# A float32 attention chain on one core: moving the first layer's softmax normalisation behind the product with the values

## The chip, the cores and the metric

The kernel runs on one core of a Trainium2 chip. The metric is the device time of one execution in microseconds (us); lower is better. Everything is float32. A large product is made of three passes of matmuls: each operand is split into a high part (type fp32r) and the low rest, and high times high, high times low and low times high are added up.

## The reference

Four sequences of 512 tokens of width 512 go through three blocks (16 tiles of 128 rows on the chip):

```python
# layer 0: grouped-query attention, 32 query heads of 16 columns, 8 key/value heads, blocks of 128 keys
attn = softmax(q @ k.T / 4 + mask)          # float32, over the 128 keys
x = layernorm((attn @ v) @ Wo + bo + x) * gamma + beta
# layers 1 and 2: x = x + cross_attention(layernorm(x), ctx)   (16 heads of 128 columns, one bias key and value)
# then the MLP:   x = x + gelu(layernorm(x) @ W1 + b1) @ W2 + b2
```

Only layer 0 is changed. Dividing the weights by their sum ahead of the product with `v` or dividing the product behind it gives the same result.

## The kernel before, in words

The 16 row tiles are worked off in two halves of 8 tiles (`hf` = 0, 1); each half goes through layer 0, the two cross-attention layers and the MLP. The program is written out by hand per engine (`@block.tensor`, `.scalar`, `.vector`, `.gpsimd`, `.sync`); each engine's queue runs strictly in the order written, and semaphores tie the queues together. No planner is involved.

**Layer 0 of a half** has 8 units (`u`), each a group of 8 heads for 4 tiles, and so 32 steps (`s` = 0 to 31, `u = s // 4`). A step is one tile with 8 heads, a block of 128 rows by 1024 weights. It passes through the engines so:

- TensorE `s0_(s)` (L647 to L661, 12 matmuls) makes the scores in PSUM banks 2 to 5, columns 0 to 255 of each. There is one such buffer, so scores `s + 1` wait for `z0` of step `s`.
- VectorE `soft0(s)` adds the mask and copies the scores to one of four SBUF buffers (L1343, semaphore `z0`), and takes the negated maximum of each head (L1348).
- ScalarE `e0(s)` (L1059) takes the exponential of the first OWN = 5 heads, one instruction each (L1064, with the maximum as bias and the sum over the row accumulated). GpSimd `sub(s)` (L415) subtracts the maximum for the other 3 heads, and ScalarE then takes their exponential in one instruction (L1067).
- VectorE `rec0(s)` sums those 3 heads (L1353) and takes the reciprocals of the 8 sums (L1358).
- GpSimd `norm(s)` multiplies all 1024 weights by the reciprocals (L422).
- TensorE `t0(s)` transposes the 8 heads (L670), waiting for `norm`; ScalarE copies them out of PSUM (L1117); TensorE `pv0(s)` multiplies by the values (L683, 16 small matmuls) into one fourth of PSUM bank 1.
- After four steps of a unit, ScalarE adds the value bias and writes the high part of the contexts (L1075), VectorE the low part (`cxlo0`, L1362).
- TensorE `out0` (L688) multiplies the contexts by `Wo` into bank 0; VectorE adds the tile to `X` (`add0`, L1310). `q0(u)` (12 matmuls, L567) makes the next units' queries, whose two parts ScalarE (L1047) and VectorE (`qlo0`, L1335) write.

What each engine does in iteration `s` of its loop is fixed by hand. TensorE: `t0(s)`, `pv0(s-1)`, `s0_(s+4)`, then the extras named for `s` in `Q_AT` and `ROWS_AT`. ScalarE: the copy of `t0(s)`, then `e0(s+3)`. VectorE: `rec0(s+1)`, `cxlo0`, `qlo0`, `soft0(s+3)`, `add0`. GpSimd: `norm(s+1)`, `sub(s+3)`, then a row of the output bias (`BO_AT`, L456) and pieces of 256 columns of the weight slabs of later stages (`SPLIT_AT`): a copy (L385) and a subtraction (L446) each.

**The end of layer 0 in a half.** TensorE fills the last four iterations with the first keys and values of layer 1. VectorE takes the statistics of the first four rows (L1373), needs a square root of ScalarE (`root`, L1082, after a load of its table), finishes the layer norm (`own`, L1409 and L1407), adds the first values' bias (L1486) and takes new statistics (L1417), and writes the low part of the last contexts (L1362). Then TensorE runs the last 12 matmuls of `last_rows0` (L703), 48 matmuls of values and the transposes of the first rows of layer 1 (L789).

## Time and profile before

| | us |
|---|---|
| runs, median of 3 | 2455.49 (2453.92 to 2456.33) |
| profiled execution: own time | 2454.8 |
| its span | 2453.0 |
| TensorE busy | 2363.4 (96%) |
| VectorE busy | 1218.1 (50%) |
| ScalarE busy | 866.1 (35%) |
| GpSimd busy | 815.1 (33%) |

The profiled execution took 1.8 us more than its span and 0.7 us less than the median. A busy share is a mean over the span. In the 40 slices of the page TensorE stands at 9 tenths nearly everywhere, but layer 0 of either half (from about 25 to 200 us and from about 1240 to 1415 us) looks different from the rest: there VectorE, ScalarE and GpSimd stand at 7 to 10 tenths. For a change in layer 0 those two stretches are to be read, not the means.

### The profile page before, as it was taken

What the parts mean: (1) busy time and instruction counts of PE and PEld (TensorE: products, weight loads), DVE (VectorE), ACT (ScalarE), POOL (GpSimd) and SP (SyncE); (2) the same over time, 40 slices, a digit from 0 to 9 for tenths busy, and PEclk for the clock granted to TensorE, in tenths of its full rate; (3) what the DMA queues carried; (4) which work ended last, traced back from release to release, by engine and by line L of the source; (5) the groups of instructions that cost most, each with busy time, mean ns of one, the idle gap of its engine ahead of it and who ended that gap; (6) DMA issues with size and microseconds to landing.
All of it is one profiled execution on the core that took longest, in us unless ns stands there. A gap on an engine that the chain in (4) does not pass through costs nothing.

```text
span 2453.0 us, 38741 instructions
## 1 busy us (share of the span) xinstructions
PE 2363.4 (96%) x14768; PEld 2033.3 (83%) x14768; DVE 1218.1 (50%) x2041; ACT 866.1 (35%) x2499; POOL 815.1 (33%) x598
## 2 busy tenths in 40 slices
PE   6888999999999999999989899999999999999999
PEld 5677888888888898878867678888888888888887
DVE  6986333334533334466679853343354333434654
ACT  6964222222422222242369542222233222223321
POOL 5974222233422322230049542223243222322100
PEclk9999999999999999999999999999999999999999
DMA  4102101012110101211320021111111111110110
GB/s 179 36 10 82 35 34 60 34 43 67 41 35 34 43 34 35 81 43 52 107 96 10 10 82 36 42 51 43 51 57 35 35 43 34 43 51 13 61 43 35
DMA packets 37765, 120.08 MB, mean 49 GB/s; under 512 B 3616, under 2 KB 3872, under 8 KB 37664
## 3 DMA queue, kind: packets, MB, share of 16 engines
q1 hardware_dynamic: 37664, 118.69, 14.0%
q8 instruction: 68, 1.11, 0.2%
q14 instruction: 33, 0.27, 0.0%
HBM read 114.48 MB, written 4.19 MB: 48 GB/s over the span
## 4 chain that ended last, share of the span: by engine, by line
PE 84%; POOL 7%; DVE 3%; ACT 2%; issue 2%; DMA 1%; SPq 0%; POOLq 0%; DVEq 0%; ACTq 0%
PE PS L567 71%; PE PS L798 5%; PE PS L814 4%; PE PS L806 2%; POOL XN L422 1%; POOL W L446 1%; ACT AT L1137 1%; POOL X L456 1%; POOL XN L415 1%; POOL HF L422 1%; POOL P0D L422 1%; POOL W L385 1%; ACT PS L1137 1%; PE PS L789 1%; PE PS L834 0%
## 5 line engine op out<-in xcount | busy, mean ns | idle before, releaser
L567 PE MATMUL PS<-AT,W 128*128 128x512 f32 x2496 | 607.5, 394 | 7.1 <-DVE AT L1431 6.0
L567 PEld LDWEIGHTS PS<-AT,W 128*128 128x128 f32 x2496 | 471.3, 190 | 111.2 <-DVE AT L1431 8.2
L485 POOL TENSOR_TENSOR PR<-PR,RC 128x512 f32<-128x512 f32 x128 | 133.3, 1041 | 979.4 <-DVE RC L1516 979.4
L1310 DVE TENSOR_TENSOR X<-PS,X 128x512 f32<-128x512 f32 x416 | 286.0, 690 | 293.8 <-PE PS L567 286.6
L567 PE MATMUL PS<-CT,W 128*128 128x512 f32 x1632 | 411.1, 401 | 10.4 <-DVE CT L1305 10.4
L567 PE MATMUL PS<-W,CX 128*128 128x512 f32 x1632 | 397.1, 397 | 7.7 <-DVE Q L1335 4.1
L567 PE MATMUL PS<-W,CT 128*128 128x256 f32 x3072 | 385.8, 284 | 0.0
L567 PEld LDWEIGHTS PS<-W,CT 128*128 128x128 f32 x3072 | 372.9, 191 | 1.3 <-issue 0.8
L567 PEld LDWEIGHTS PS<-W,CX 128*128 128x128 f32 x1632 | 299.8, 188 | 75.0 <-issue 8.3
L567 PEld LDWEIGHTS PS<-CT,W 128*128 128x128 f32 x1632 | 300.5, 190 | 69.8 <-issue 11.0
L1164 ACT ACTIVATE CX<-PS,VEC 128x512 fp32r<-128x512 f32 x128 | 88.0, 688 | 660.7 <-PE PS L814 660.7
L1541 DVE TENSOR_TENSOR V<-PS,BVR 128x512 f32<-128x512 f32 x124 | 85.5, 691 | 397.1 <-PE PS L567 397.1
L1153 ACT ACTIVATE PR<-PS,MX 128x129 f32<-128x129 f32 x512 | 181.7, 370 | 179.9 <-DVE MX L1510 179.9
L378 POOL TENSOR_TENSOR W<-RAW,W 128x1024 fp32r<-128x1024 f32 (+1 forms) x101 | 240.3, 2379 | 8.4
L385 POOL TENSOR_SCALAR W<-RAW 128x1024 fp32r<-128x1024 f32 (+2 forms) x149 | 135.1, 907 | 263.3 <-PE PS L567 250.4
L1147 ACT ACTIVATE Q<-PS,BQS 128x512 f32<-128x512 f32 x128 | 88.0, 688 | 345.0 <-PE PS L567 345.0
L567 PE MATMUL PS<-W,HB 128*128 128x512 f32 x768 | 180.2, 390 | 0.1
L567 PEld LDWEIGHTS PS<-W,HB 128*128 128x128 f32 x768 | 143.8, 188 | 30.7 <-DVE X L1310 1.0
L1547 DVE SCALAR_TENSOR_TENSOR CX<-PS,VEC,CX 128x512 fp32r<-128x512 f32 x128 | 96.1, 751 | 131.5 <-ACT CX L1164 131.2
L798 PE MATMUL PS<-K,Q 128*128 128x129 f32 x1024 | 136.0, 276 | 2.6 <-ACT Q L1147 2.6
L814 PE MATMUL PS<-PT,V 128*128 128x128 f32 x1024 | 135.1, 275 | 1.4 <-ACT PT L1159 1.4
L814 PEld LDWEIGHTS PS<-PT,V 128*128 128x128 f32 x1024 | 129.3, 191 | 6.5 <-ACT PT L1159 1.8
(108 smaller groups left out, 2450.5 us busy)
## 6 DMA issues: line engine op xcount, KB each, us to landing
RAW<-in_wq SPq DMA_DIRECT2D x44, 512.0 KB, 4.3
RAW<-in_wo SPq DMA_DIRECT2D x44, 512.0 KB, 3.3
RAW<-in_wk SPq DMA_DIRECT2D x40, 512.0 KB, 3.2
RAW<-in_wv SPq DMA_DIRECT2D x40, 512.0 KB, 3.5
raw_c<-in_cT SPq DMA_DIRECT2D x8, 512.0 KB, 5.8
raw_x<-in_xT SPq DMA_DIRECT2D x8, 512.0 KB, 6.3
BVR<-in_bv_rows SPq DMA_DIRECT2D x8, 512.0 KB, 3.7
X<-in_x SPq DMA_DIRECT2D x4, 1024.0 KB, 11.5
```

The source lines that it names most:

```text
L378: eng.tensor_tensor(W[:, n, 1, 0:width], RAW[:, n, 0:width], W[:, n, 0, 0:width].bitcast(F32), ALU.subtract).then_inc(w_ready[n], 1)
L385: return nc.gpsimd.tensor_scalar(out, in_, 1.0, 0.0, ALU.mult, ALU.add)
L485: nc.gpsimd.tensor_tensor(PR[:, :, 0:P], PR[:, :, 0:P], RC[:, 0, 0:BT].unsqueeze(2).to_broadcast([P, BT, P]), ALU.mult).then_inc(norm_done, 1)
L567: ins = nc.tensor.matmul(out, lhs(c, a), rhs(c, b), start=(k == 0), stop=(k == total - 1))
L798: ins = nc.tensor.matmul(PS[:, BS + b // 2, b % 2 * 256:b % 2 * 256 + T1], Q[:, b * P:(b + 1) * P], K[:, h, b, 0:T1], start=True, stop=True)
L814: ins = nc.tensor.matmul(PS[:, BPV, b * P:(b + 1) * P], V[:, tb, b, h * P:(h + 1) * P], PT[:, b * P:(b + 1) * P], start=True, stop=True)
L1147: nc.scalar.activation(Q[:], PS[:, BA, :], ACT.Identity, bias=BQS[:, bass.ds(ly * H1 + head, 1)], scale=K1 ** -0.5).then_inc(q_ev, 1)
L1153: ins = nc.scalar.activation(PR[:, b, 0:T1], PS[:, BS + b // 2, b % 2 * 256:b % 2 * 256 + T1], ACT.Exp, bias=MX[:, 0, b:b + 1], accum_out= ...
L1164: nc.scalar.activation(CX[:, h, 0, :], PS[:, BPV, :], ACT.Identity, bias=VEC[:, bass.ds(cols + g * 2 + (COL_BIASV + h), 1)]).then_inc(cx_h ...
L1310: V_.tensor_tensor(X[:, tile, :], PS[:, bank, :], X[:, tile, :], ALU.add).then_inc(done, 1)
L1541: V_.tensor_tensor(V[:, tb, 2 * i:2 * i + 2, :], PS[:, BC + i, :].rearrange("p (b d) -> p b d", d=256), BVR[:, bass.ds(g * 256, 256)].unsq ...
L1547: V_.scalar_tensor_tensor(CX[:, h, 1, :], PS[:, BPV, :], VEC[:, bass.ds(cols + g * 2 + (COL_BIASV + h), 1)], CX[:, h, 0, :].bitcast(F32), ...
```

## The change

OWN goes from 5 to 4. `norm` is gone. TensorE transposes the weights as soon as `e0` has made them. GpSimd gets `half(s)`, which adds the two halves of each of the last 4 heads into 64 columns, and VectorE sums those. The reciprocals are written 16 times each, as 128 columns (`RC0`), TensorE transposes them (`rt0`) into columns 256 to 383 of a score bank, and once a unit VectorE multiplies the contexts by them (`cxnorm0`). ScalarE only copies the contexts out of PSUM (`cxraw0`); GpSimd splits them into two parts (`context`), and for the last unit ScalarE and VectorE do. The value bias is added to the values instead. VectorE's loop runs `rec0(s)` at its end instead of `rec0(s+1)` at its start, and adds a row between the two instructions of `soft0`. The tables of the extras are laid out anew; the first keys and values of layer 1, the statistics and the root each come one iteration later.

```diff
@@ -39,18 +39,18 @@
...
-OWN = 5
+OWN = 4
 BUFS0 = 4
 Q_AT = {0: 2, 3: 3, 8: 4, 12: 5, 16: 6, 20: 7}
-SPLIT_AT = {0: (3, (0,)), 1: (3, (1,)), 2: (3, (2,)), 3: (3, (3,)), 4: (0, (0,)), 5: (0, (1,)), 6: (0, (2,)), 7: (0, (3,)),
-            12: (2, (0,)), 13: (2, (1,)), 14: (2, (2,)), 15: (2, (3,)), 20: (1, (0, 1)), 21: (1, (2, 3)),
-            22: (3, (0,)), 23: (3, (1,)), 24: (3, (2, 3)), 25: (0, (0,)), 26: (0, (1,)), 27: (0, (2,)), 28: (0, (3,))}
+SPLIT_AT = {0: (3, (0,)), 1: (3, (1,)), 2: (3, (2,)), 3: (3, (3,)), 4: (0, (0, 1)), 6: (0, (2,)), 7: (0, (3,)),
+            11: (2, (0,)), 13: (2, (1,)), 15: (2, (2,)), 16: (2, (3,)), 17: (1, (0,)), 18: (1, (1,)), 20: (1, (2,)), 21: (1, (3,)),
+            24: (3, (0, 1)), 25: (3, (2, 3)), 26: (0, (0,)), 27: (0, (1,)), 28: (0, (2,)), 29: (0, (3,))}
 PIECES = sum(len(parts) for _, parts in SPLIT_AT.values())
-BO_AT = {8: 0, 9: 1, 10: 2, 11: 3, 16: 4, 17: 5, 18: 6, 19: 7}
-ROWS_AT = {9: (0, 0), 10: (0, 1), 11: (0, 2), 13: (0, 3), 17: (1, 0), 18: (1, 1), 19: (1, 2), 21: (1, 3),
-           25: (2, 0), 26: (2, 1), 27: (2, 2), 28: (2, 3)}
+BO_AT = {8: 0, 9: 1, 10: 2, 12: 3, 13: 4, 14: 5, 19: 6, 20: 7}
+ROWS_AT = {10: (0, 0), 11: (0, 1), 14: (0, 2), 15: (0, 3), 18: (1, 0), 19: (1, 1), 22: (1, 2), 23: (1, 3),
+           26: (2, 0), 27: (2, 1), 28: (2, 2), 29: (2, 3)}
...
@@ -109,7 +109,7 @@
...
-        SUM0 = sb("SUM0", [P, 2, 8])
+        SUM0 = sb("SUM0", [P, 4, 8])
...
@@ -129,12 +129,15 @@
...
+        CXF = in_arena("CXF", [P, 3, 2, BTOK], F32, 36864)
...
               HF[:].rearrange("p a n -> p (a n)"), P0D[:]]
         PTB = in_arena("PTB", [P, 2, 1024], F32, 49152)
...
@@ -173,8 +176,9 @@
         vt_ps, vt_ev, v0_ps, v0_ev, q0_ps, q0_hi, q0_lo = (sem(n) for n in ("vt_ps", "vt_ev", "v0_ps", "v0_ev", "q0_ps", "q0_hi", "q0_lo"))
         k0_ps, k0_hi, k0_lo = (sem(n) for n in ("k0_ps", "k0_hi", "k0_lo"))
-        s0_ps, z0, max0, sub0, exp0, sum0, rc0, norm0 = (sem(n) for n in ("s0_ps", "z0", "max0", "sub0", "exp0", "sum0", "rc0", "norm0"))
+        s0_ps, z0, max0, sub0, exp0, sum0, rc0, half0 = (sem(n) for n in ("s0_ps", "z0", "max0", "sub0", "exp0", "sum0", "rc0", "half0"))
         t0_ps, t0_ev, pv0_ps = (sem(n) for n in ("t0_ps", "t0_ev", "pv0_ps"))
+        rt_ps, cx0_raw, cx0_n = sem("rt_ps"), sem("cx0_raw"), sem("cx0_n")
         cx0_hi, cx0_lo, o0_ps = (sem(n) for n in ("cx0_hi", "cx0_lo", "o0_ps"))
         own_mid, own_done = sem("own_mid"), sem("own_done")
@@ -415,20 +419,29 @@
...
-                def norm(s):
-                    pool.wait_ge(rc0, hf * STEPS0 + (s + 1))
-                    z = P0[s % BUFS0].rearrange("p (h t) -> p h t", t=P)
-                    nc.gpsimd.tensor_tensor(z, z, RC[:, s % 2, :].unsqueeze(2).to_broadcast([P, KV0, P]),
-                                            ALU.mult).then_inc(norm0, 1)
+                def half(s):
+                    pool.wait_ge(exp0, hf * STEPS0 + (s + 1))
+                    if s >= 2:
+                        pool.wait_ge(rc0, hf * STEPS0 + (s - 1))
+                    z = P0[s % BUFS0].rearrange("p (h t) -> p h t", t=P)[:, OWN:KV0, :]
+                    nc.gpsimd.tensor_tensor(HS[:, s % 2, :, :], z[:, :, 0:P // 2], z[:, :, P // 2:P], ALU.add).then_inc(half0, 1)
+                def context(u):
+                    pool.wait_ge(cx0_n, hf * UNITS0 + (u + 1))
+                    copy_hi(CX0[:, u % 3, 0, :], CXF[:, u % 3, 1, :]).then_inc(cx0_hi, 1)
+                    pool.wait_ge(cx0_hi, hf * UNITS0 + (u + 1))
+                    nc.gpsimd.tensor_tensor(CX0[:, u % 3, 1, :], CXF[:, u % 3, 1, :], CX0[:, u % 3, 0, :].bitcast(F32),
+                                            ALU.subtract).then_inc(cx0_lo, 1)
...
@@ -464,15 +477,17 @@
...
-                norm(0)
                 sub(2)
+                half(0)
                 for s in range(STEPS0):
-                    if s + 1 < STEPS0:
-                        norm(s + 1)
                     if s == STEPS0 - 2:
                         sub_rows(0, 0)
                     if s + 3 < STEPS0:
                         sub(s + 3)
+                    if s + 1 < STEPS0:
+                        half(s + 1)
+                    if s % 4 == 1 and s > 1:
+                        context(s // 4 - 1)
                     if s in BO_AT:
                         add_bo_tile(BO_AT[s])
                     if s in SPLIT_AT:
@@ -661,7 +676,7 @@
...
                 def t0(s):
-                    pe.wait_ge(norm0, s0 + (s + 1))
+                    pe.wait_ge(exp0, s0 + (s + 1))
...
@@ -677,13 +692,19 @@
...
-                        pe.wait_ge(cx0_lo, u0 + u)
+                        pe.wait_ge(cx0_raw, u0 + u)
                     for e in range(2):
...
+                def rt0(s, bank, col):
+                    pe.wait_ge(rc0, s0 + (s + 1))
+                    nc.tensor.transpose(PS[:, bank, col:col + P], RC0[:, s % 4, :],
+                                        IDENT[:]).then_inc(rt_ps, 1)
...
@@ -754,25 +775,33 @@
...
                     if s:
                         pv0(s - 1)
+                    if s and s <= STEPS0 - 4:
+                        pe.wait_ge(z0, s0 + (s + 4))
+                        if s % 4 == 1 and s > 1:
+                            pe.wait_ge(cx0_n, u0 + s // 4)
+                        rt0(s - 1, B0 + (s - 1) % 4, 256)
                     if s + 4 < STEPS0:
                         s0_(s + 4)
                     if s in Q_AT:
...
                         out0(s)
-                    if s == STEPS0 - 4:
-                        pe.wait_ge(z0, s0 + STEPS0)
+                    if s == STEPS0 - 3:
+                        pe.wait_ge(cx0_n, u0 + UNITS0 - 1)
                         keys(n1, 0, 0, w1, BS)
-                    if s == STEPS0 - 3:
+                    if s == STEPS0 - 2:
                         values(n1, 0, w1, None, (0, 1))
-                    if s == STEPS0 - 2:
+                    if s == STEPS0 - 1:
                         values(n1, 0, w1, None, (2, 3))
-                    if s == STEPS0 - 1:
-                        keys(n1, 0, 1, w1, BS + 1)
+                keys(n1, 0, 1, w1, BS + 1)
                 pe.wait_ge(w_ready[3], nq + G0)
+                pe.wait_ge(cx0_lo, u0 + UNITS0 - 1)
                 last_rows0(0, 0)
+                pe.wait_ge(xadd, x0 + 3 * BT)
                 last_rows0(1, 0)
                 pv0(STEPS0 - 1)
+                for t in range(BT):
+                    rt0(STEPS0 - BT + t, BPV, t * P)
...
@@ -1039,7 +1068,7 @@
                 def vtev0(tb):
                     act.wait_ge(vt_ps, hf * TB + (tb + 1))
-                    nc.scalar.activation(VT[:, tb, :], PS[:, BB, :], ACT.Copy).then_inc(vt_ev, 1)
+                    nc.scalar.activation(VT[:, tb, :], PS[:, BB, :], ACT.Identity, bias=VEC[:, COL_BV0:COL_BV0 + 1]).then_inc(vt_ev, 1)
                 def qev0(u):
                     act.wait_ge(q0_ps, u0 + (u + 1))
@@ -1058,22 +1087,21 @@
...
                 def e0(s):
                     act.wait_ge(max0, s0 + (s + 1))
-                    if s >= 2:
-                        act.wait_ge(rc0, s0 + (s - 1))
+                    if s >= 4:
+                        act.wait_ge(rc0, s0 + (s - 3))
...
-                def cxhi0(u):
+                def cxraw0(u):
...
-                    nc.scalar.activation(CX0[:, u % 3, 0, :], PS[:, BB, :], ACT.Identity,
-                                         bias=VEC[:, COL_BV0:COL_BV0 + 1]).then_inc(cx0_hi, 1)
+                    nc.scalar.activation(CXF[:, u % 3, 1, :], PS[:, BB, :], ACT.Copy).then_inc(cx0_raw, 1)
...
@@ -1117,15 +1145,17 @@
...
-                        cxhi0(s // 4 - 1)
+                        cxraw0(s // 4 - 1)
                     if s + 3 < STEPS0:
                         e0(s + 3)
-                    if s == STEPS0 - 4:
+                    if s == STEPS0 - 3:
                         first_keys(0, BS)
-                    if s == 30:
+                    if s == 31:
                         root(hf * 8)
                 first_keys(1, BS + 1)
-                cxhi0(UNITS0 - 1)
+                cxraw0(UNITS0 - 1)
+                act.wait_ge(cx0_n, u0 + UNITS0)
+                nc.scalar.activation(CX0[:, (UNITS0 - 1) % 3, 0, :], CXF[:, (UNITS0 - 1) % 3, 1, :], ACT.Copy).then_inc(cx0_hi, 1)
                 root(hf * 8 + 1)
...
@@ -1335,7 +1365,7 @@
...
-                def soft0(s):
+                def soft0(s, row=None):
...
@@ -1344,23 +1374,43 @@
...
+                    if row is not None:
+                        row0(row)
                     dve.wait_ge(z0, s0 + (s + 1))
                     V_.tensor_reduce(MX[:, s % BUFS0, :], P0[s % BUFS0].rearrange("p (h t) -> p h t", t=P),
                                      AXX, ALU.max, negate=True).then_inc(max0, 1)
+                def row0(s):
+                    n, t = ROWS_AT[s]
+                    if n < 2:
+                        dve.wait_ge(bo_tile, hf * SEQ + (n * BT + t + 1))
+                    add0(n, t, BA)
                 def rec0(s):
                     dve.wait_ge(exp0, s0 + (s + 1))
-                    V_.tensor_reduce(SUM0[:, s % 2, OWN:KV0], P0[s % BUFS0].rearrange("p (h t) -> p h t", t=P)[:, OWN:KV0, :],
-                                     AXX, ALU.add).then_inc(sum0, 1)
-                    if s >= 2:
-                        dve.wait_ge(norm0, s0 + (s - 1))
+                    dve.wait_ge(half0, s0 + (s + 1))
+                    V_.tensor_reduce(SUM0[:, s % 4, OWN:KV0], HS[:, s % 2, :, :], AXX, ALU.add).then_inc(sum0, 1)
+                    if s >= 4:
+                        dve.wait_ge(rt_ps, s0 + (s - 3))
                     dve.wait_ge(sum0, s0 + (s + 1))
-                    V_.reciprocal(RC[:, s % 2, :], SUM0[:, s % 2, :]).then_inc(rc0, 1)
-                def cxlo0(u):
-                    dve.wait_ge(cx0_hi, u0 + (u + 1))
-                    V_.scalar_tensor_tensor(CX0[:, u % 3, 1, :], PS[:, BB, :], VEC[:, COL_BV0:COL_BV0 + 1],
-                                            CX0[:, u % 3, 0, :].bitcast(F32), ALU.add, ALU.subtract).then_inc(cx0_lo, 1)
+                    V_.reciprocal(RC0[:, s % 4, :].rearrange("p (h d) -> p h d", d=HD0),
+                                  SUM0[:, s % 4, :].unsqueeze(2).to_broadcast([P, KV0, HD0])).then_inc(rc0, 1)
+                def cxnorm0(u):
+                    dve.wait_ge(cx0_raw, u0 + (u + 1))
+                    if u < UNITS0 - 2:
+                        dve.wait_ge(s0_ps, s0 + (4 * u + 9))
+                    else:
+                        dve.wait_ge(rt_ps, s0 + (4 * u + 4))
+                    rt = PS[:, B0:B0 + 4, 256:256 + P] if u < UNITS0 - 1 else PS[:, BPV, :].rearrange("p (b t) -> p b t", t=P)
+                    cx = CXF[:, u % 3, 1, :].rearrange("p (b t) -> p b t", t=P)
+                    V_.tensor_tensor(cx, rt, cx, ALU.mult).then_inc(cx0_n, 1)
+                def last_cxlo0():
+                    u = UNITS0 - 1
+                    dve.wait_ge(cx0_hi, u0 + UNITS0)
+                    V_.tensor_tensor(CX0[:, u % 3, 1, :], CXF[:, u % 3, 1, :], CX0[:, u % 3, 0, :].bitcast(F32),
+                                     ALU.subtract).then_inc(cx0_lo, 1)
...
@@ -1450,7 +1500,6 @@
                 if hf:
                     last_down((0, 1))
                 soft0(1)
-                rec0(0)
                 if hf:
                     last_down((2, 3))
                 soft0(2)
@@ -1458,23 +1507,20 @@
...
                 for s in range(STEPS0):
-                    if s + 1 < STEPS0:
-                        rec0(s + 1)
                     if s % 4 == 1 and s > 1:
-                        cxlo0(s // 4 - 1)
+                        cxnorm0(s // 4 - 1)
                     if s - 2 in Q_AT:
                         qlo0(Q_AT[s - 2])
+                    row = s - 1 if s - 1 in ROWS_AT else None
                     if s + 3 < STEPS0:
-                        soft0(s + 3)
-                    if s - 1 in ROWS_AT:
-                        n, t = ROWS_AT[s - 1]
-                        if n < 2:
-                            dve.wait_ge(bo_tile, hf * SEQ + (n * BT + t + 1))
-                        add0(n, t, BA)
-                    if s == 29:
+                        soft0(s + 3, row)
+                    elif row is not None:
+                        row0(row)
+                    rec0(s)
+                    if s == 30:
                         stats(0, range(BT), x0 + 9)
                         variances(hf * 8, 1e-6)
-                    if s == 30:
+                    if s == 31:
                         roots(hf * 8)
                         own(0, 0)
...
@@ -1488,9 +1534,11 @@
...
-                own_stats(0, range(2))
-                cxlo0(UNITS0 - 1)
-                own_stats(0, range(2, BT))
+                own_stats(0, range(1))
+                cxnorm0(UNITS0 - 1)
+                own_stats(0, range(1, 3))
+                last_cxlo0()
+                own_stats(0, range(3, BT))
...
```

Left out of the diff: the limits 25 in `pieces` (L427, L431), which become 26. `HS` and `RC0` lie in a part of `BVR` that layer 0 does not use.

## Rows read from the trace of the kernel before

**Rows 1.** Busy times, first and second half, from scores 4 to scores 31.
```profile
core 0: us, PE busy (x) PEld busy (x) DVE busy (x) ACT busy (x) POOL busy (x), PEclk, DMA share, GB/s
45.97:154.75 108.78, 93.09 (x1117) 70.91 (x1117) 98.47 (x133) 97.30 (x337) 104.90 (x107) 0.98 0.07 26
1259.92:1369.38 109.46, 93.72 (x1117) 71.43 (x1117) 98.50 (x133) 97.34 (x337) 104.90 (x107) 0.98 0.07 26
```

**Rows 2.** Chain that ended last, second half, one stretch: start, us, what.
```profile
1321.94 0.37 POOL W L385
...
1322.40 0.73 POOL W L446
1323.14 1.86 POOL XN L422
1324.99 0.79 POOL P0D L415
1325.78 1.25 POOL X L456
```

**Rows 3.** Timeline of VectorE, first half: start, us, engine, line, operation.
```profile
97.79 0.54 DVE L1353 TENSOR_REDUCE SUM<-P0D 128x3 f32<-128x384 f32 x1
98.44 0.20 DVE L1358 RECIPROCAL RC<-SUM 128x8 f32<-128x8 f32 x1
98.56 0.70 DVE L1335 SCALAR_TENSOR_TENSOR Q<-PS,VEC,Q 128x512 fp32r<-128x512 f32 x1
99.22 1.23 DVE L1343 TENSOR_TENSOR XN<-PS,BIASVR 128x1024 f32<-128x1024 f32 x1
100.48 1.22 DVE L1348 TENSOR_REDUCE MX<-XN 128x8 f32<-128x1024 f32 x1
101.62 0.68 DVE L1310 TENSOR_TENSOR X<-PS,X 128x512 f32<-128x512 f32 x1
```

**Rows 4.** Single lines of VectorE: count, then minimum, median and maximum in ns.
```profile
L1358 DVE RECIPROCAL RC<-SUM x64: 202/203/205, 31.2 to 1379.2; 128x8 f32<-128x8 f32 x64
...
L1516 DVE RECIPROCAL RC<-SUM x128: 172/178/180, 201.4 to 2259.3; 128x4 f32<-128x4 f32 x128
...
L1392 DVE TENSOR_TENSOR NT<-NT,RS x16: 161/163/164, 170.6 to 2280.4; 128x4 f32<-128x4 f32 x16
```

**Rows 5.** Groups of GpSimd, whole program: busy us, mean ns of one.
```profile
L485 POOL TENSOR_TENSOR PR<-PR,RC 128x512 f32<-128x512 f32 x128 | 133.3, 1041 | 979.4 <-DVE RC L1516 979.4
...
L446 POOL TENSOR_TENSOR W<-RAW,W 128x256 fp32r<-128x256 f32 x48 | 35.2, 734 | 4.0
...
L378 POOL TENSOR_TENSOR W<-RAW,W 128x512 fp32r<-128x512 f32 x2 | 2.6, 1282 | 0.2
L385 POOL TENSOR_SCALAR W<-RAW 128x512 fp32r<-128x512 f32 x2 | 1.2, 614 | 4.6 <-DMA RAW<-in_wk 4.6
```

**Rows 6.** Timeline of the first half: scores 4 and 31, then the end.
```profile
45.97 0.77 PE L658 MATMUL PS<-KZ,Q 32*128 32x256 f32 x12 [4.45 <-DVE P0D L1343]
...
154.13 0.62 PE L658 MATMUL PS<-KZ,Q 32*128 32x256 f32 x12
...
154.68 1.66 PE L567 MATMUL PS<-W,CX 128*128 128x512 f32 x6
...
166.71 1.04 PE L670 MATMUL PS<-IDENT,HF 128*128 128x128 f32 x8
...
167.68 0.65 PE L683 MATMUL PS<-PTB,VP 128*32 128x128 f32 x16
...
170.36 0.18 DVE L1391 RECIPROCAL RS<-SD 128x4 f32<-128x4 f32 x1 [5.60 <-ACT SD L1082]
...
177.79 1.28 DVE L1417 BATCH_NORM_STATS2 BNS<-X 128x6 f32<-128x512 f32 x2
...
178.99 0.74 DVE L1362 SCALAR_TENSOR_TENSOR CX<-PS,VEC,CX 128x512 fp32r<-128x512 f32 x1
...
179.78 3.02 PE L703 MATMUL PS<-W,CX 128*128 128x512 f32 x12 [0.46 <-DVE CX L1362]
```

8 lines of the change are left out of this document (5 added, 3 removed).

## The prediction

> **What bounds the kernel now.** I read the page's 40 slices first: TensorE is at 9 tenths outside layer 0, so nothing there can move. Then the busy times of the stretch from scores 4 to scores 31, 27 iterations of the loop: 108.8 us in the first half, 109.5 in the second [rows 1]. GpSimd is busy 104.9 of it, VectorE 98.5, ScalarE 97.3, TensorE 93.1. Last the chain of waits there, which runs along GpSimd without a break [rows 2]: `norm` 1.86, `sub` 0.79, a bias row 1.25, a piece 0.46 + 0.74 = 1.20 from start to start. 27 x 2.65 + 22 pieces x 1.20 + 8 rows x 1.25 = 108.0 us: the loop is as long as GpSimd's list. What the change takes from GpSimd is therefore worth something, but only until the next engine is reached, and VectorE has 10 us of air in 109.
>
> **GpSimd after.** `norm` goes. `sub` has 512 columns, as the multiplication at L485, 1.04 us; `half` reads two operands for 256 outputs, as L446, 0.73; `context` is a copy and a subtraction of 512 columns, 0.61 + 1.28 = 1.89 [rows 5]. 27 x 1.77 + 6 x 1.89 + 26.4 + 10 = 95.5 us, 12.5 less. It stops being the bound.
>
> **VectorE after.** From start to start [rows 3]: mask addition 1.26, maximum 1.14, sum of three heads 0.65, reciprocals 0.12, a row's addition about 0.60, `qlo0` 0.66. Three edits count.
> - The sum falls from 384 columns to 256. Sum and maximum give (1.22 - 0.54) us / 640 = 1.06 ns a column, so 0.65 - 0.14 = 0.51.
> - A row between mask addition and maximum fills a wait of about 0.1: 0.50 instead of 0.60. `cxnorm0` reads PSUM and SBUF with 512 columns as L1310: 0.60. `cxlo0` goes.
> - **The reciprocals are written as 128 columns instead of 8**, and this decides. No row shows 128. Two sizes are shown: 8 columns take 203 ns, 4 take 178, and an ordinary instruction of 4 columns 163 [rows 4]. That is 25 ns for 4 columns, 6.25 ns each, and it fits the third row: 163 + 4 x (6.25 - 1.06) = 184. So 128 columns take 0.203 + 120 x 6.25 ns = 0.95 us, 0.75 more than now, 0.87 from start to start. The ends: with the 1.06 ns of sum and maximum it would be 0.33 us; if the whole duration grew with the columns, 16 x 0.203 = 3.25 us. I take 0.95, since it rests on the same instruction; the scatter of the two sizes (180 to 202, 172 to 205 ns) allows 5.5 to 8.3 ns a column, 0.86 to 1.20 us.
>
> The Trainium skill (Vector Engine (DVE) Microarchitecture Reference, section 5.2 Measured stream behaviour on trn2) speaks otherwise: built-in operations of one or two sources scale with 1.04 ns a column. By that rule the reciprocals cost 0.33 us and the change gains; it is the first rival. The skill (VectorE: DVE Perf Modes, First, the fixed hardware budget) also says that the reciprocal is an iterated division with a repeat count of 8, without a price; the rows agree that it is dearer than other work.
>
> Sum of the 27 iterations: 27 x (1.26 + 1.14 + 0.51 + 0.87) = 102.1; 8 rows x 0.50 = 4.0 (those of steps 10 to 23; the later ones fall behind); 6 `cxnorm0` x 0.60 = 3.6; 6 `qlo0` x 0.66 = 4.0. Together 113.7 us between the mask additions of steps 3 and 30. Scores 4 and 31 follow these alike, and scores 31 take 0.6: **114.3 us**, where GpSimd's list took 108.8. VectorE becomes the bound.
>
> **The others.** TensorE gets 27 transposes of 1.04/8 = 0.13 [rows 6], at most 96.6 us. Its waits for `z0` ahead of `rt0` are those that the scores had anyway, and `rc0` of the step before is older than that `z0` in VectorE's new order. ScalarE loses a head's exponential per step and stays under 97.3. The value bias costs nothing: the same copy of PSUM, under TensorE's work.
>
> **A stall at step 26.** `out0(26)` needs the unit 5 contexts and the second `Wo` slab, and GpSimd has both in iteration 25. Counted from the maximum of step 28: `sub` 1.04, `half` 0.73, `context` 1.89, two pieces 2.40 = 6.1 us. TensorE is there earlier: VectorE's rest of the iteration 1.38, mask addition 1.23, start 0.15, scores 30 in 0.6 = 3.4. So TensorE waits 2.7 us, with `t0(27)`, `pv0(26)` and scores 31 queued behind, and behind scores 31 the end of layer 0 is TensorE's own list, so it is lost: 117.0 us. Bounds 0 (GpSimd's two pieces early) and 5 (if it comes late to iteration 25).
>
> **Ahead of the loop.** `rec0(1)` (0.65 + 0.12) no longer stands before the mask addition of step 3: -0.8 us.
>
> **The end.** From the end of scores 31 (154.75) to the last `last_rows0` (179.78) it is 25.0 us [rows 6]: 13.0 to the end of `t0(30)` at 167.75, full of TensorE's work, then 12.0 through the root of ScalarE, VectorE's layer norm from 170.36, two statistics and `cxlo0`. The root now stands behind `t0(31)`: TensorE has one more `out0` (1.6), one more `t0` and `pv0` (166.71 to 168.33, 1.6) and an `rt0` (0.1) ahead of it, 16.3. Behind it VectorE has one more statistic (0.64) and `cxnorm0` (0.68) ahead of the low part: 13.3. Together 29.6, **+4.6 us**. At least it is +2.2, the `out0` and five transposes more. Nothing behind absorbs it, since values and transposes follow on TensorE.
>
> **Sum.** First half 117.0 - 108.8 - 0.8 + 4.6 = +12.0; second half 117.0 - 109.5 - 0.8 + 4.6 = +11.3. The profiled execution's 2454.8 us become 2478.1; the median lies 0.7 higher. I predict 2478.
>
> **Rivals.**
> 1. *Cheap reciprocals* (0.33 us); this one ends on the other side. VectorE's iteration is 1.26 + 1.14 + 0.51 + 0.25 = 3.16, the stretch 85.3 + 11.6 + 0.6 = 97.5, the stall 3.3, so 100.8; -8.0 and -8.7, with -0.8 and +4.6 each: -9.1 in all, 2446. VectorE 97, TensorE 96.6 and GpSimd 95.5 would be so near each other with one buffer of scores that some would be lost: 2446 to 2454. For it: the other operations' slope. Against: both sizes of the reciprocal in the trace. It decides below 0.60 us for 128 columns: 27 x 2 x (0.95 - 0.60) = 19 us, and the stalls, would bring the sum near zero. 14 in 100, 4 of them within 0.2%.
> 2. *Only the loop pays.* VectorE bound as forecast, but no stall at step 26 and the end at its least: 2478 - 5.4 - 4.8 = 2468. For it: GpSimd has light iterations 22 and 23 ahead. Against: the pieces stand in the queue behind `sub`, which waits for VectorE's maximum whatever GpSimd has spare. 15 in 100.
> 3. *GpSimd again*, by being late with `sub` after heavy iterations such as 13 (`context`, a row, a piece: 6.1 us), so that ScalarE and `t0` slip. An iteration of VectorE is 3.8 to 4.4, the next ones of GpSimd 3.0, so it catches up in two; at 1 us in each of the four heaviest, 8 in all: 2486. 7 in 100.
>
> The forecast has 64 in 100. A measurement can tell about 0.2%, 5 us, from no change: faster 0.10, the same 0.04, slower 0.86. Range: below, 0.86 us for the reciprocals (-5), no stall (-5.4) and the least end (-4.8): 2463; above, 1.20 us (+13.5) and a stall of 5 (+4.6): 2496. I take 2462 to 2496; rival 1 stays outside.
>
> **What would show it.** The reciprocal's group with 64 of about 950 ns; VectorE busy over 95% between scores 4 and 31, a stretch of about 117 us, the chain there on VectorE's lines and hardly on GpSimd's; `out0` of step 26 waiting for GpSimd; the last `last_rows0` about 29.6 us behind scores 31; GpSimd's busy time down by some 35 us. A reciprocal of 330 ns, or a stretch under 109 us, proves me wrong.

## The result, and the profile after

The changed kernel takes **2481.18 us** (median of 4 runs, 2479.4 to 2484.75) against 2455.91 us (median of 4, 2453.92 to 2456.51) for the kernel before: a ratio of 1.0107, 95% interval 1.0091 to 1.0123. It is slower by 25.3 us; the forecast was slower too, 2478 (range 2462 to 2496). The profiled execution has 2481.43 us and a span of 2479.6.

The busy times of the profile's page and, last, each engine's share of the chain of work that ended last:

```profile
PE 2379.8 (96%) x14832; PEld 2042.2 (82%) x14832; DVE 1253.5 (51%) x2043; ACT 852.6 (34%) x2373; POOL 782.5 (32%) x626
...
PE 85%; DVE 5%; issue 4%; POOL 3%; ACT 3%; DMA 0%; SPq 0%; POOLq 0%; DVEq 0%; ACTq 0%
```

GpSimd's busy time fell by 32.6 us, VectorE's rose by 35.4. Busy times by stretch, changed kernel (stretch, its length, then busy us of PE, PEld, DVE, ACT, POOL; clock, DMA share, GB/s): from scores 4 to scores 31 in either half, which answer to [rows 1]; a part of the first one; the end of the first half; its last 12 matmuls.

```profile
47.71:165.91 118.20, 101.52 (x1138) 75.82 (x1138) 111.07 (x132) 91.44 (x285) 92.12 (x118) 0.94 0.07 24
1273.76:1391.42 117.66, 101.31 (x1138) 75.77 (x1138) 111.01 (x132) 91.36 (x285) 92.13 (x118) 0.96 0.07 24
...
156.00:166.00 10.00, 7.53 (x57) 5.57 (x58) 6.78 (x10) 4.54 (x14) 7.61 (x12) 0.57 0.16 53
165.91:194.92 29.01, 26.15 (x219) 21.46 (x220) 23.87 (x44) 12.53 (x30) 11.27 (x14) 1.00 0.00 1
194.92:199.53 4.61, 4.61 (x14) 3.66 (x15) 3.71 (x13) 0.21 (x1) 0.00 (x0) 0.63 0.01 2
```

VectorE is now the fullest engine of the loop and GpSimd, which had 104.9 of 108.8 us, has 13 us less. Instructions of VectorE in one iteration, changed kernel, beside [rows 3]:

```profile
97.13 1.21 DVE L1380 TENSOR_REDUCE MX<-P0D 128x8 f32<-128x1024 f32 x1
98.25 0.41 DVE L1392 TENSOR_REDUCE SUM<-BVR 128x4 f32<-128x256 f32 x1
98.76 0.95 DVE L1396 RECIPROCAL BVR<-SUM 128x128 f32<-128x128 f32 x1
99.63 0.63 DVE L1407 TENSOR_TENSOR CXF<-PS,CXF 128x512 f32<-128x512 f32 x1
100.18 1.21 DVE L1373 TENSOR_TENSOR XN<-PS,BIASVR 128x1024 f32<-128x1024 f32 x1
```

Where 0.20 us of reciprocal stood, 0.95 us stand, 0.87 from start to start. TensorE around step 26 in the first half:

```profile
152.48 0.33 PE L706 MATMUL PS<-IDENT,BVR 128*128 128x128 f32 x1 [2.29 <-DVE XN L1373]
...
154.32 1.08 PE L698 MATMUL PS<-PTB,VP 128*32 128x128 f32 x16
156.19 0.47 PE L706 MATMUL PS<-IDENT,BVR 128*128 128x128 f32 x1 [0.79 <-DVE XN L1373]
156.59 1.01 PE L673 MATMUL PS<-KZ,Q 32*128 32x256 f32 x12
159.89 2.90 PE L582 MATMUL PS<-W,CX 128*128 128x512 f32 x6 [2.28 <-issue]
162.59 1.91 PE L685 MATMUL PS<-IDENT,P0D 128*128 128x128 f32 x8
```

and GpSimd's last piece of the slab before it:

```profile
159.06 0.73 POOL L459 TENSOR_TENSOR W<-RAW,W 128x256 fp32r<-128x256 f32 x1
```

`out0` starts when that piece ends, after a wait of 2.28 us. TensorE had already idled for VectorE's mask additions (2.29 and 0.79 us), and its granted clock from 156 to 166 us is 0.57, so most of that stretch ran at the lower of its two levels: the same 6 matmuls took 2.90 us where they take 1.66 at the higher level, scores 1.01 instead of 0.63. The lower level set in ahead of the wait for GpSimd: the clock is 0.50 from 154.5 us on, behind the wait of 2.29 us.

The chain of waits at the end of the first half, to be laid beside [rows 6]:

```profile
181.79 0.02 ACT PTB L1145
...
182.84 1.28 ACT L1110
...
184.37 0.19 DVE RS L1441
...
192.49 0.59 DVE CXF L1407
...
194.28 0.60 DVE CX L1412
194.88 0.04 issue
194.92 4.61 PE PS L724 x12
```

It is the forecast chain: `t0(31)`, ScalarE's root with its table, VectorE's layer norm, `cxnorm0`, low part, last rows.

**Where the time went.** From scores 1 on, against before: scores 1 to 4 -0.7 us (18.28 instead of 18.98), first loop +9.4, its end +4.0 (29.0 instead of 25.0), its 12 last matmuls +1.6 (4.61 instead of 3.02), second half +8.2, +4.0 and +1.6. That is 28.1. Between the halves the changed kernel was 2.9 us quicker (1074.2 instead of 1077.1 from the last rows to the second half's scores 4, in which lies the second -0.7), it began 2.4 us later, and the part behind the second half was 1.0 us shorter: 26.6 us, the difference of the spans. What made the part between the halves quicker was not taken apart. The late beginning belongs to this execution and not to the change: scores 1 start at 29.4 us here and at 27.1 in the runs 2, 4 and 7 below. Run 4 is the same code up to there; its first load of `in_wq` took 7.62 us instead of 8.47, and 12 matmuls behind it 3.02 us instead of 4.61.

### The profile page after: what moved, and what is told of

Same layout as the page of the kernel before. It is cut to its first block, busy times and chain, and to the rows that moved or that the text cites. A ratio compares the mean times of both kernels' runs of the same rounds, so it can differ in the third digit from the quotient of the medians.

```text
span 2479.6 us, 38963 instructions
## 1 busy us (share of the span) xinstructions
PE 2379.8 (96%) x14832; PEld 2042.2 (82%) x14832; DVE 1253.5 (51%) x2043; ACT 852.6 (34%) x2373; POOL 782.5 (32%) x626
## 4 chain that ended last, share of the span: by engine, by line
PE 85%; DVE 5%; issue 4%; POOL 3%; ACT 3%; DMA 0%; SPq 0%; POOLq 0%; DVEq 0%; ACTq 0%
PE PS L582 72%; PE PS L827 5%; PE PS L843 4%; PE PS L835 2%; POOL BVR L428 1%; ACT AT L1167 1%; ACT PS L1167 1%; DVE XN L1373 1%; PE PS L685 1%; POOL W L459 0%; POOL XN L419 0%; DVE AT L1481 0%; PE PS L673 0%; PE PS L818 0%; DVE X L1459 0%
```

## The experiments

Twelve kernels. The stretch always means the start of scores 4 to the end of scores 31, the end from there to the start of the last 12 matmuls. Runs 1 to 7 and 9 are single executions, run 8 has 4, runs 10 and 11 have 11 and run 12 has 10; the four of the changed kernel lie 5 us apart, so of a single run a few us of the total say nothing, and the stretches say more.

**1. The price of the reciprocal by itself**, in the kernel before, ahead of VectorE's first work:

```diff
+                    for n in (4, 8, 16, 32, 64, 128):
+                        V_.reciprocal(PTB[:, 0, n:2 * n], VEC[:, 0:n])
+                    V_.reciprocal(PTB[:, 0, 256:384].rearrange("p (h d) -> p h d", d=HD0), VEC[:, 0:8].unsqueeze(2).to_broadcast([P, KV0, HD0]))
+                    V_.tensor_copy(PTB[:, 0, 384:512], VEC[:, 0:128])
+                    V_.tensor_copy(PTB[:, 0, 512:640].rearrange("p (h d) -> p h d", d=HD0), VEC[:, 0:8].unsqueeze(2).to_broadcast([P, KV0, HD0]))
```

> The kernel before, with nine extra VectorE instructions ahead of its first work, in time in which VectorE waits for the first loads: reciprocals of 4, 8, 16, 32, 64 and 128 columns, one of 8 columns read 16 times each into 128, and two copies into 128 columns (of 128, and of 8 read 16 times each). Theory A (a reciprocal costs 6.25 ns a column): 178, 203, 253, 353, 553 and 953 ns, and the spread one 953 too. Rival B (about 1.06 ns a column behind the first few): 128 columns in 330 ns. Rival C (the stride of zero is what costs): 128 plain columns in 330 ns and the spread one near 950. The copies about 290 ns each by the slope of the other instructions. Total time as before, 2455 us, within 3.

Groups of VectorE at the start of the span (busy us, mean ns):

```profile
L1437 DVE RECIPROCAL PTB<-VEC 128x128 f32<-128x128 f32 x1 | 0.9, 896 | 0.0
L1438 DVE RECIPROCAL PTB<-VEC 128x128 f32<-128x128 f32 x1 | 0.9, 896 | 0.0
L1437 DVE RECIPROCAL PTB<-VEC 128x64 f32<-128x64 f32 x1 | 0.5, 496 | 0.0
L1440 DVE COPY PTB<-VEC 128x128 f32<-128x128 f32 x1 | 0.2, 216 | 0.0
L1437 DVE RECIPROCAL PTB<-VEC 128x16 f32<-128x16 f32 x1 | 0.2, 203 | 0.0
L1437 DVE RECIPROCAL PTB<-VEC 128x8 f32<-128x8 f32 x1 | 0.2, 172 | 0.0
```

L1437 is the plain reciprocal and L1438 the one that reads 8 numbers 16 times each: both take 896 ns, so the repeated reading costs nothing. (896 - 496) / 64 = 6.25 ns a column, the slope of the forecast to the digit. It does not hold down to the smallest sizes: 4 columns took 178 ns, 8 took 172 and 16 took 203. So the 25 ns between the forecast's two rows, of 4 and of 8 columns at two different places of the program, were not the price of four columns, and it was luck that their slope was right. The plain copy took 164 ns and the spreading one 216, less than the 290 expected, with GpSimd idle; run 7 comes back to that. The whole took 2455.04 us, as expected.

**2. The reciprocal at 8 columns, nothing spread.** 120 of the 128 columns keep old numbers, so the contexts are not normalised.

```diff
+            nc.gpsimd.memset(BVR[:, 1536:2048], 1.0)
...
-                    V_.reciprocal(RC0[:, s % 4, :].rearrange("p (h d) -> p h d", d=HD0),
-                                  SUM0[:, s % 4, :].unsqueeze(2).to_broadcast([P, KV0, HD0])).then_inc(rc0, 1)
+                    V_.reciprocal(RC0[:, s % 4, 0:KV0], SUM0[:, s % 4, :]).then_inc(rc0, 1)
```

> The changed kernel, with reciprocals of only the 8 sums, written to the first 8 columns of the slot; the other 120 keep an old content, so the contexts are not normalised rightly, and everything else (transposes, waits, sizes) is as in the changed kernel. Theory A (the 128 columns of reciprocals make VectorE the bound and are the whole loss of the loop): VectorE's iteration 3.16 us, from scores 4 to scores 31 about 100 us instead of 118.2, total 2446 us (up to 2454 where engines of nearly equal load lose some to each other). Rival B (the new couplings, rt0 ahead of the scores and rec0 behind GpSimd's half, hold the loop): the stretch stays over 112 us and the total over 2468.

2461.6 us, 19.6 less than the changed kernel; the two stretches together are 19.5 us shorter. So the width is the whole loss of the loop, and what is left of the 25.3 us lies outside it. The two stretches, then `out0(26)`:

```profile
45.41:153.79 108.38, 99.58 (x1138) 75.05 (x1138) 92.48 (x132) 90.39 (x285) 91.52 (x117) 0.97 0.08 26
1261.56:1369.51 107.95, 99.10 (x1138) 74.65 (x1138) 92.22 (x132) 90.32 (x285) 90.99 (x117) 0.97 0.08 26
```

```profile
148.31 2.64 PE L583 MATMUL PS<-W,CX 128*128 128x512 f32 x6 [3.96 <-issue]
```

108.4 us, neither the forecast 100.8 nor over 112 as rival B has it. No engine is full, since they take turns: in units with `q0` or `out0` in every step TensorE has a list of its own (5.24 + 2.41 + 3.88 + 3.85 = 15.4 us for four steps), in the others VectorE holds it up (about 3.0 a step), and the stall at step 26 grew to 3.96 us: GpSimd's list of that iteration takes 6.0 us from its `sub` to the last piece as before (142.19 to 148.21 us), while TensorE is ready for `out0` 2.2 us after that `sub` begins and not 3.8.

**3. The wide reciprocal alone, in the kernel before.**

```diff
-                    nc.gpsimd.tensor_tensor(z, z, RC[:, s % 2, :].unsqueeze(2).to_broadcast([P, KV0, P]),
+                    nc.gpsimd.tensor_tensor(z, z, RCW[:, s % 2, :].rearrange("p (h d) -> p h d", d=HD0)[:, :, 0:1].to_broadcast([P, KV0, P]),
...
-                    V_.reciprocal(RC[:, s % 2, :], SUM0[:, s % 2, :]).then_inc(rc0, 1)
+                    V_.reciprocal(RCW[:, s % 2, :].rearrange("p (h d) -> p h d", d=HD0),
+                                  SUM0[:, s % 2, :].unsqueeze(2).to_broadcast([P, KV0, HD0])).then_inc(rc0, 1)
```

> The kernel before, with nothing changed but its reciprocals, which are written as 128 columns (each sum 16 times); GpSimd's normalisation reads every 16th. Theory A: VectorE needs 27 x (1.26 + 1.14 + 0.65 + 0.87) + 14 = 119.8 us from scores 4 to scores 31 instead of GpSimd's 108.8, so +11.6 in the first half, +11 in the second, and about 1 more at either end: 2479 us. Rival B (VectorE has room, as its 10 us of idle time suggest, and GpSimd stays the bound): under 2460 us.

2485.53 us, 31.9 slower and 6.5 above the expectation: this one edit costs more than the whole change. The stretches are 121.9 and 121.6 us instead of the expected 119.8, VectorE busy 114.8. Single steps took up to 7.2 us where TensorE waited for VectorE's part of the queries (2.21 us at 90.60) and GpSimd's `norm`, which waits for each reciprocal, came late as well; how much of the loss is that was not taken apart.

**4. The root before ScalarE's copy of `t0(31)`.**

```diff
+                    if s == 31:
+                        root(hf * 8)
                     act.wait_ge(t0_ps, s0 + (s + 1))
...
-                    if s == 31:
-                        root(hf * 8)
```

> The changed kernel, with ScalarE's root of the first layer norm ahead of the copy of t0(31) instead of behind it. Theory A (the end of layer 0 is the chain t0(31), root, layer norm, contexts): the root ends 3.4 us earlier, the last 12 matmuls of last_rows0 start 2.1 us earlier in either half, since then TensorE's own list ends last; 2477 us. Rival B (TensorE's own list sets the end already): no change, 2481 us.

2471.68 us. The end is 27.4 us instead of 29.0 in both halves, the loop is unchanged (118.2), and

```profile
190.19 3.03 PE L724 MATMUL PS<-W,CX 128*128 128x512 f32 x12 [1.25 <-DVE CX L1412]
```

the last 12 matmuls take 3.03 us behind a wait of 1.25, where they took 4.61 behind one of 2.86. So 3.2 us a half, 6.4 in all, more than the 2.1 a half of theory A, which had the start of those matmuls and not their slow clock; the start itself moved by 1.6. Most of the rest is the beginning: this execution began 2.4 us sooner.

**5. GpSimd's slab pieces at steps 23 and 24** instead of 24 and 25.

```diff
-            24: (3, (0, 1)), 25: (3, (2, 3)), 26: (0, (0,)), 27: (0, (1,)), 28: (0, (2,)), 29: (0, (3,))}
+            23: (3, (0, 1)), 24: (3, (2, 3)), 26: (0, (0,)), 27: (0, (1,)), 28: (0, (2,)), 29: (0, (3,))}
```

> The changed kernel with one edit: GpSimd's two last pieces of the fourth slab of Wo are taken one step earlier (steps 23 and 24 instead of 24 and 25), so that out0(26), which waited until GpSimd's piece ended (157.6 to 159.9 us, 2.28 us), finds its slab ready. Theory A (my forecast's term: the wait at step 26 is a late slab of GpSimd, and nothing else is late there): that wait is gone in both halves, scores 30 to scores 31 falls from 8.7 and 8.2 us to about 4, by the wait of 2.3 and by the slow clock behind it; the stretch from scores 4 to scores 31 falls from 118.2 and 117.7 to about 114; total 2481 - 8 = 2473. Rival B (the clock falls because of the 2.29 us wait for VectorE's additions at 150.2 us, ahead of out0): only the 2.3 us go, the matmuls of that step keep the slow clock, stretch 116, total 2477. Rival C (the slab's bytes or VectorE are late as well): nothing changes.

2474.79 us; stretches 115.3 and 115.0. TensorE, first half:

```profile
149.69 0.33 PE L706 MATMUL PS<-IDENT,BVR 128*128 128x128 f32 x1 [2.29 <-DVE XN L1373]
...
153.41 0.33 PE L706 MATMUL PS<-IDENT,BVR 128*128 128x128 f32 x1 [1.23 <-DVE XN L1373]
...
154.70 2.74 PE L582 MATMUL PS<-W,CX 128*128 128x512 f32 x6 [0.41 <-POOL CX L435]
```

The wait of 2.28 is down to 0.41 us and now ends with GpSimd's `context`, but a longer wait for VectorE stands ahead of it, and in this half the matmuls still ran slowly (2.74 us), as B has it: scores 30 to 31 took 5.9 us instead of 8.7. In the second half the same waits stand there and the matmuls ran fast (1.65 us), as A has it: 4.3 us instead of 8.2. Its stretch is shorter by 2.6 us only, since behind scores 4 twelve matmuls ran slowly, 5.49 us instead of 4.22, which the edit doesn't touch. So the slab was the late one, and what its removal gives back, 2.8 and 3.9 us at the place itself, depends on the clock.

**6. ScalarE spreads the 8 reciprocals.**

```diff
-        RC = sb("RC", [P, 2, 8])
+        RC = sb("RC", [P, 4, 8])
...
+                    nc.scalar.activation(RC0[:, s % 4, :].rearrange("p (h d) -> p h d", d=HD0),
+                                         RC[:, s % 4, :].unsqueeze(2).to_broadcast([P, KV0, HD0]), ACT.Copy).then_inc(rx0, 1)
...
-                    V_.reciprocal(RC0[:, s % 4, :].rearrange("p (h d) -> p h d", d=HD0),
-                                  SUM0[:, s % 4, :].unsqueeze(2).to_broadcast([P, KV0, HD0])).then_inc(rc0, 1)
+                    V_.reciprocal(RC[:, s % 4, :], SUM0[:, s % 4, :]).then_inc(rc0, 1)
```

> The changed kernel, with VectorE's reciprocal back at 8 columns (172 to 178 ns) and ScalarE spreading them over the 128 columns by a copy of its own (one more ScalarE instruction a step, some 0.25 us) behind the step's other work. The result is what the changed kernel computes. Theory A (the reciprocal's width on VectorE is what the change lost in the loop; ScalarE has room, 91 of 118 us busy): it comes out as the kernel with 8-column reciprocals and nothing spread, 2461.6, within 3 us; stretch scores 4 to 31 about 108.4 in both halves, end 29. Rival B (ScalarE's wait for the reciprocal holds back its exponentials): stretch over 112, total over 2468.

2484.55 us, a miss by 23. Against run 2 the loop explains 9 of them (111.8 and 113.4 us; TensorE waits for ScalarE's copy 24 times, 15.3 us in all). The rest was lost where nothing had been edited: 1081.5 us between the halves instead of 1074.2, and as much again behind the second. Run 9 looks for it.

**7. VectorE spreads them with a copy** (reciprocal into `RC`, wait, then `V_.tensor_copy` into `RC0`).

> The changed kernel with VectorE's reciprocal at 8 columns and a VectorE copy that spreads them (216 ns in the run of sizes) behind a wait for it. The result is what the changed kernel computes. From start to start VectorE's two instructions cost 0.17 to 0.2 + 0.22 and about 0.1 for the wait, 0.45 to 0.5 against 0.87 to 0.95 for the wide one: the iteration falls from 3.78 to about 3.35. By the two narrower points (108.4 us at 3.0, 118.2 at 3.78) the stretch is about 113, total 2481.4 - 2 x 5.2 = 2471. Rival (TensorE's list with the stalls at steps 26 to 31 sets the narrow version, VectorE only the wide one): 109, 2463.

2479.28 us, only 2 less than the wide reciprocal and 8 above the expectation; stretches 115.6 and 117.0. VectorE's copies and GpSimd's instructions at the same time:

```profile
101.84 1.29 POOL L470 TENSOR_TENSOR X<-X,BO 128x512 f32<-128x512 f32 x1
103.05 0.23 DVE L1399 COPY BVR<-RC 128x128 f32<-128x128 f32 x1
...
58.11 1.04 POOL L420 TENSOR_TENSOR HF<-HF,MX 128x512 f32<-128x512 f32 x1 [0.68 <-DVE MX L1381]
58.63 0.60 DVE L1399 COPY BVR<-RC 128x128 f32<-128x128 f32 x1
```

The copy that begins as GpSimd ends has 0.23 us. The other began 0.52 us before GpSimd's instruction ended (59.15) and ended 0.08 behind it. All 64 copies: 226 ns at least, 535 in the middle, 1118 at most; 57 of them end 0.07 to 0.09 us behind the GpSimd instruction in which they began, and the other 7, which began in its last 0.09 us or with none running, take 0.23 us. So the copy stands until GpSimd's instruction is over. The Trainium skill (SBUF — State Buffer, section SBUF: two separate sides) has this as a rule: VectorE and GpSimd share a pair of ports under an exclusive lock, which a copy in a two-port mode needs. The trace agrees on the blocking; that this copy runs in such a mode is not shown by it.

**8. Runs 4, 5 and 6 together.**

> Three edits together on the changed kernel: 8-column reciprocals with ScalarE's spreading copy, GpSimd's slab pieces at steps 23 and 24, and ScalarE's square root ahead of its copy of the last unit's reciprocals. From the sums of the single runs: 2481.3 - 19.6 (reciprocals) - 6.3 (root) = 2455.4, and the slab: the narrow kernel still has 9.4 and 9.2 us between scores 30 and 31 where 4 would do, so 2 x 5 less: 2445. Rival (the steps 26 to 31 are held by VectorE's additions or by the clock, not by GpSimd): 2455. Below 2453.6 it beats the kernel before.

2470.88 us (ratio to before 1.0067, interval 1.005 to 1.0084); stretches 108.9 and 110.6. That is 26 above the expectation and 16 above its rival. It has the larger `RC` too.

**9. Only the larger `RC`.**

```diff
-        RC = sb("RC", [P, 2, 8])
+        RC = sb("RC", [P, 4, 8])
```

> The changed kernel with the buffer RC declared as 4 x 8 instead of 2 x 8 numbers per partition, and nothing else: the buffers declared behind it lie 64 bytes further on. In the kernels with ScalarE's spreading copy, which have this larger buffer, the work between the first half's last rows and the second half's scores 4, in which nothing was edited, took 1081.5 us instead of 1074.2, with TensorE's matmuls of the same form up to 6 ns longer each (396 instead of 390 ns for those on HB), and the same came a second time in the second half: 14 us in all. Theory S (the place of the buffers in memory does it): this kernel shows it too, 1081.5 us in that stretch and 2481.4 + 14 = 2495 in all. Rival T (the extra work or semaphore on ScalarE does it, or the state of that chip): 1074.2 us and 2481.

2496.8 us: 15.6 slower for a declaration. From the first half's last rows to the second half's scores 4 it takes 1081.5 us, and TensorE's groups there are

```profile
L582 PE MATMUL PS<-AT,W 128*128 128x512 f32 x1176 | 282.7, 391 | 3.8 <-DVE AT L1481 3.8
L582 PE MATMUL PS<-W,CX 128*128 128x512 f32 x744 | 181.8, 398 | 0.8 <-DVE CX L1595 0.6 <-DVE V L1589 0.2
L582 PE MATMUL PS<-W,HB 128*128 128x512 f32 x384 | 92.5, 396 | 0.0
L863 PE MATMUL PS<-W,CX 128*128 128x512 f32 x24 | 7.3, 455 | 0.1
```

and in the changed kernel, same lines:

```profile
L582 PE MATMUL PS<-AT,W 128*128 128x512 f32 x1176 | 282.6, 391 | 3.9 <-DVE AT L1481 3.9
L582 PE MATMUL PS<-W,CX 128*128 128x512 f32 x744 | 178.9, 396 | 0.8 <-DVE CX L1595 0.6 <-DVE V L1589 0.2
L582 PE MATMUL PS<-W,HB 128*128 128x512 f32 x384 | 90.3, 390 | 0.1
L863 PE MATMUL PS<-W,CX 128*128 128x512 f32 x24 | 6.2, 401 | 0.1
```

The three lower groups take 6.2 us of the 7.3 more, the first none. The part behind the second half is longer by 6.5 us. So theory S: runs 6 and 8 carried some 14 us that are none of their edits. Without them they would be, by this estimate, at about 2470 and 2457, and run 8 near its rival's 2455.

**10. A reduction spreads them**, with the edits of runs 4 and 5:

```diff
+                    V_.reciprocal(RC[:, s % 2, :], SUM0[:, s % 4, :]).then_inc(rcn0, 1)
+                    dve.wait_ge(rcn0, s0 + (s + 1))
+                    V_.tensor_reduce(RC0[:, s % 4, :].rearrange("p (h d) -> p h d", d=HD0),
+                                     RC[:, s % 2, :].unsqueeze(2).unsqueeze(3).to_broadcast([P, KV0, HD0, 1]),
+                                     AXX, ALU.max).then_inc(rc0, 1)
```

> The changed kernel with three edits: VectorE's reciprocals at 8 columns, spread over 128 by a VectorE reduction over an axis of one element (a form that reads one operand, where the copy took 536 ns whenever GpSimd was in an instruction); GpSimd's slab pieces at steps 23 and 24; ScalarE's root ahead of its copy at step 31. The result is what the changed kernel computes. A reduction of 128 columns should be about 0.28 us, from 1.22 us for 1024 and 0.41 for 256 (1.05 ns a column). Theory A (width of the reciprocal and GpSimd's hold on the copy were the loop's loss): the iteration falls to about 3.3 us, the stretch from scores 4 to scores 31 to about 107 us, end 27.4 with 3.0 for the last matmuls, total 2451 to 2456. Rival B (the reduction is held by GpSimd as the copy was, 0.54 us): stretch about 113, total 2466.

2453.62 us (11 runs), ratio to before 0.9996, interval 0.9987 to 1.0005. The new line, all its instructions (minimum, median, maximum ns), and the first stretch:

```profile
L1399 DVE TENSOR_REDUCE BVR<-RC x64: 285/286/289, 47.3 to 1380.9; 128x128 f32<-128x128 f32 x64
```

```profile
45.63:154.11 108.48, 99.91 (x1138) 74.87 (x1138) 100.05 (x160) 91.06 (x285) 91.68 (x118) 0.97 0.08 26
```

GpSimd never held it. Where VectorE binds, a step takes 3.34 us instead of 3.72, and the end is what theory A said (27.4 and 3.0 us); the stretch is 108.5 and 107.9 us, near 107; in the second half 1.3 us of it are the same twelve slow matmuls behind scores 4 as in run 5. All of the change's loss is undone, and the kernel stands level with the one before.

**11. The end re-ordered on top of that**: `pv0(31)` and the four last transposes ahead of the next half's first keys on TensorE, `cxraw0` and the high part ahead of `first_keys` on ScalarE.

> The kernel of e10 with the end of each half re-ordered as well: TensorE's last values and the transposes of the last four reciprocals go before the next half's first keys, and ScalarE copies the last contexts and writes their rounded half before its share of those keys. Theory A (the last contexts' chain ends the half: reciprocal, transposes, normalising product, rounded half, rest, 12 matmuls): the end is shorter by 0.5 to 1 us in each half than in e10, 1 to 2 us in all. Rival (TensorE has that much other work there anyway, so that the chain is covered): same as e10 within 0.5 us. A second rival (moved forward, TensorE waits for the last step's exponentials and transposes with nothing else to do): slower than e10 by up to 2 us.

```profile
177.30 5.62 PE L725 MATMUL PS<-W,CX 128*128 128x512 f32 x24
```

All last rows run without a wait, and from scores 31 to their end it takes 28.9 us in either half instead of 30.4 and 30.5. That is 3 us in all, more than theory A has. The whole shows nothing of it: 2453.85 us, ratio 0.9995 (0.9986 to 1.0004). In the two traces most of it is lost again behind the last rows, where the two programs are the same: 0.9 us between the halves and 1.5 behind the second. The gain is in the trace of the end and not shown in the time.

**12. The kernel of run 10 with the large buffer 256 bytes further on.**

```diff
-        at = (nc.sbuf_base + 127) // 128 * 128
-        sb("arena", [P, ARENA // 4 + 24])
+        at = (nc.sbuf_base + 127) // 128 * 128 + 256
+        sb("arena", [P, ARENA // 4 + 24 + 64])
```

> The kernel of e10 with the large common buffer (scores' keys, contexts, later Q, K, V, contexts and HB) begun at byte 166528 of each partition instead of 166272, the small buffers ahead of it untouched. In the run of the larger RC that buffer began at 166400, 128 bytes further on, and the small ones behind RC moved by 64 bytes; it cost 15.4 us, most of it in TensorE's matmuls that read that buffer (HB 390 to 396 ns, contexts 396 to 398, the turn's contexts 401 to 455), while those that read the sources stayed at 391. Theory P (what counts is the place modulo 256 bytes; 166272 and 166528 are alike): 2453.6 as e10, and 1075 us from the end of the first half's last rows to the second half's scores 4. Rival Q (each displacement of that buffer costs, or its place in a longer period does): 1080 us or more there and 2465 or more in all. Third case (the small buffers did it, not the large one): 2453.6 too; only the next stage's matmuls on HB, 390 ns, would then be no evidence for P.

2454.38 us, ratio 0.9997 (0.9988 to 1.0007), the matmuls on HB at 390 ns: as run 10. That excludes Q, that any displacement of this buffer costs. P and the third case both stand. The slowed matmuls are those that read the large buffer, which speaks for P, but moving it alone by 128 bytes wasn't tried.

## Why the prediction was right

**The reciprocals** (0.95 us, 0.87 from start to start): 953 ns, 0.87. This term decided, and its size was right. The step to it was lucky: its slope came from a difference that run 1 doesn't find between 4 and 8 columns, and its start of 203 ns belongs to a reciprocal that waits for the sum (alone, run 1 has 172 and 896 ns). The 1.04 ns a column of the Trainium skill (Vector Engine (DVE) Microarchitecture Reference, section 5.2 Measured stream behaviour on trn2), the page beside rival 1, is near what the maximum and the sum show here, (1.22 - 0.41) us / 768 = 1.05 ns, but the reciprocal has 6.25.

**GpSimd's list** (95.5 us, 12.5 less): 92.1 busy, 12.8 less; `sub` 1.04, `half` 0.73, `context` 0.62 + 1.28. Right.

**VectorE's list** (114.3 without the stall, the stretch 117.0): 118.2 and 117.7. VectorE was busy 94% of it (111.1 of 118.2), just under the 95% named as the sign. The chain of waits through the first stretch has 42 us on VectorE's lines, 45 on TensorE's and none on GpSimd's (the rest is "issue"): VectorE took GpSimd's place, but in the steps with `q0` it is TensorE's list that binds, which a sum of VectorE's list alone doesn't see.

**TensorE** (at most 96.6 us): 101.5 and 101.3, too low. A transpose of the reciprocals takes 0.33 us, and the scores start 0.26 us behind it, twice the 0.13 of the sum; the slow clock adds to it (run 2, with a clock of 0.97, has 99.6 and 99.1). It did no harm to the forecast, as TensorE was not taken for the bound, but it does to rival 1.

**The stall at step 26** (2.7 us, bounds 0 and 5): the mechanism was right, a wait of 2.28 us that ends with GpSimd's piece; run 5 got back 2.8 and 3.9 us there. Mis-sized was what comes with it: the granted clock of 0.57 from 156 to 166 us, which was in no term. Scores 30 to 31 took 8.7 and 8.2 us where other steps with an `out0` take 4.0, so by this estimate 4.7 and 4.2 us were lost instead of 2.7, and the rest of the stretch took 113.5 us instead of 114.3: two errors that partly cancel.

**Ahead of the loop** (-0.8): -0.7.

**The end** (+4.6, 29.6 us): 29.0 us, +4.0, by the chain named; run 4 shows that the root's place behind `t0(31)` is 1.6 of it. The forecast ended this term at the start of the last 12 matmuls and gave them their old 3.0 us. They took 4.6, +1.6 a half: with a granted clock of 0.63 behind a wait of 2.86 us. This term was missing, 3.2 us in all.

**The sum.** The profiled execution took 2481.4 us, 3.3 more than the 2478.1 of the sum. That this is as much as the missing term is luck. The loops took 1.9 us more than forecast, the last matmuls 3.2 and this execution's beginning 2.4; the two ends took 1.2 less, and the parts ahead of, between and behind the halves together 3.0 less.

**The rivals.** Rival 1's price was refuted by run 1, and run 2, which grants it even more than its price, ends at 2461.6, not at 2446 nor within the 2454 that it allowed for engines of nearly equal load. So the rival was wrong in its own working: 100.8 us for the stretch took VectorE's sum alone, where TensorE's units of 15.4 us and the grown stall bind in turn. By that run the change would have been no gain as it is written even with cheap reciprocals. It took three edits (run 10) to come level. Rival 2 falls with the stall seen. Rival 3 does too: in the first stretch GpSimd idles 31 us ahead of `sub`, waiting for the maximum, and ScalarE waited for `sub` only twice, 2.9 us in all.
